# Layer norm, residual and layer-1 steps one per 128 rows, waits per bank, weight preparation spread through batch 0, new orders

## The chip, the cores and the metric

One core of one Trainium2 chip runs the kernel. The metric is the time of one execution on the device in microseconds, median of three runs. The engines are TensorE (PE; its weight loads are PEld), VectorE (DVE), ScalarE (ACT), GpSimd (POOL) and SyncE (SP), which issues the loads and stores. Each works through its own queue in order and they meet in semaphores.

## The reference, cut to what matters

Two cross-attention layers over eight batches, all in float32. x is 8 x 512 x 256, ctx 8 x 1601 x 128.

```python
# layer 0: softmax over the QUERIES (axis 1), then residual and layer norm
q = x @ Wq + bq;  k = ctx @ Wk + bk;  v = ctx @ Wv + bv
w = softmax(q @ k.T * scale, axis=1)
x = w @ v + x
x = (x - mean(x)) * rsqrt(var(x) + 1e-6) * gamma + beta
# layer 1: softmax over the KEYS (axis -1), output projection, residual
Q = x @ Wq + bq;  K = ctx @ Wk + bk;  V = ctx @ Wv + bv
out = x + (softmax(Q @ K.T * scale, axis=-1) @ V) @ Wo + bo
```

## The kernel before, in words

The projections are folded into products of weights, made once: layer 0's in `pre0`, layer 1's in `pre1`. The keys are the raw context, 13 tiles of up to 128 rows (the last has 65). Most products are made three times: an operand is split in a high half (a cast on ScalarE) and a low half (a subtraction on VectorE or GpSimd), and `split3` adds lo x hi, hi x lo and hi x hi.

Layer 0, per batch, over key tiles i = 0..12: `scores0` (TensorE), `max0` (VectorE, adds the bias and takes the row minimum of the negated scores), `exp0` (ScalarE), `recip0` (VectorE), `norm0` (ScalarE), `p0_high` (ScalarE), `p0_low` and `sum_weights` (GpSimd), `weigh0` (TensorE, accumulates in one bank). Then `weighed0`/`at0_low` split the result, `sum_rows0` gives the sum of weights per query, and for query rows: `bias_x0`, `predict`, `residual0`, `moments0`, `rsqrt_var`, `normalised`. The normalised x goes through `turn_y`, `y_turned`, `project_q1`, `q1_high`, `q1_low`.

Layer 1, per batch, over four tiles t of 128 queries: `scores1` (four chunks of 402 keys, one PSUM bank each), `rowmax1` twice, `bias1_of` (needs `bias_row1`, a product of the normalised x and a vector, one per 128 rows), `exp1` twice. When all four are done, over the 13 key tiles: `turn_p1`, `p1_turned`, `p1_low`, `weigh1`. Then `weighed1`, `project_out`, `residual1` (GpSimd) and `finish` (VectorE), and SyncE stores in two halves.

What sets the order: four lists written out by hand, one per engine. A pass of `body` runs a list with three batches in flight: c (beginning layer 0), a (layer 0 into the layer norm) and b (layer 1). `run` unrolls this over the batches, with `pre0` before the first pass and `pre1` before the second. PSUM has eight banks: `ps_l0` (four, layer 0's scores, accumulator and one for everything else) and `ps_s1` (four, layer 1). Layer 1's chunk 0 of a batch waits for the last `finish` of the batch before (line 528), and later tiles wait until the exps of the tile before have read the banks. In the last batch, tiles alternate between `ps_s1` and `ps_l0`, which layer 0 no longer needs (lines 277 and 530):

```python
return (ps_l0 if last(b) and t % 2 else ps_s1)[:].rearrange("p (k m) -> p k m", m=BANK)
before = t - 2 if last(b) else t - 1
```

The places that the change and the prediction speak of: `pre1` at lines 628 (TensorE), 810 (ScalarE), 1008 (VectorE); `scores1` 523; `bias_x0` 887; `normalised` 924; `bias_row1` 933; `finish` 971; `residual1` 1072; the loads of x and ctx 410 to 414. The helpers read in the profile as: L432, L433, L434 the three products of `split3`; L546 `turn_p1`; L872 `max0`; L736 `exp0`; L742 `norm0`; L750 `p0_high`; L1069 `p0_low`; L1062 `sum_weights`; L779 `exp1`; L951 `rowmax1`; L962 `bias1_of`; L938 `bias_row1`; L944 `q1_low`; L978 `finish`.

Of the kernel before, what the change touches and what calls it, by code (L numbers as in the profile page):

```python
# [98 lines left out]

def xattn_kernel(nc, x, ctx, wq0, bq0, wk0, bk0, wv0, bv0, gamma, beta,  # L100
# [10 lines left out]
    R0 = 4
# [1 line left out]
    SPLIT = tuple(range(MT))

    def ring0(i):

# [1016 lines left out]
```

## Time and profile before

| | us |
|---|---|
| median of 3 runs (lowest, highest) | 513.74 (513.39, 514.05) |
| the profiled execution | 513.53 |
| its span | 511.7 |
| TensorE busy | 464.3 (91%) |
| VectorE busy | 387.2 (76%) |
| ScalarE busy | 385.2 (75%) |
| GpSimd busy | 346.2 (68%) |
| mean granted clock of TensorE, share of full | 0.983 |

Busy time counts an engine's instructions; waits and the issue of transfers are not in it. The profiled execution is 1.8 us longer than its span. The eight batches overlap, so that the middle of the program repeats one pattern per batch, and only the start and the end differ from it.

### The profile page before, as it was taken

The page shows a single profiled execution, that of the slowest core. Times are in us where ns is not written, and L with a number is a line of the kernel's source. Part 1 is how long each engine was busy: PE and PEld are TensorE (multiplying, and loading weights), DVE is VectorE, ACT ScalarE, POOL GpSimd, SP SyncE. Part 2 cuts the span into 40 slices and gives each one's busy share as a digit, 9 for nine tenths or more (in the row PEclk, how much of TensorE's full clock was granted, in tenths as well). Part 3 has the DMA queues.
Part 4 walks back from the last instruction along what each step waited for, and adds up shares of the span by engine and source line. Part 5 has one row for each costly group of instructions (what it writes and reads, how often), then busy time and mean ns, then how long its engine had stood idle before and what let it go on. Part 6 is the DMA issues. An engine that isn't in the chain of part 4 may idle for free.

```text
span 511.7 us, 7981 instructions
## 1 busy us (share of the span) xinstructions
PE 464.3 (91%) x2426; PEld 381.0 (74%) x2426; DVE 387.2 (76%) x920; ACT 385.2 (75%) x798; POOL 346.2 (68%) x319
## 2 busy tenths in 40 slices
...
GB/s 241 114 0 1 1 106 0 2 2 0 7 141 2 1 1 146 3 0 1 33 115 1 1 2 147 1 0 1 66 83 0 2 3 41 0 1 10 34 0 42
DMA packets 23897, 17.31 MB, mean 34 GB/s; under 512 B 1055, under 2 KB 23854, under 8 KB 23854
## 3 DMA queue, kind: packets, MB, share of 16 engines
...
q10 hardware_dynamic: 4, 0.00, 0.0%
...
## 4 chain that ended last, share of the span: by engine, by line
PE 41%; DVE 36%; ACT 8%; issue 8%; DMA 4%; POOL 2%; SPq 0%; DVEq 0%; POOLq 0%; ACTq 0%
DVE p1T_lo L884 7%; PE ps_s L432 5%; DVE xr L938 5%; PE ps_l L432 5%; PE ps_l L433 5%; PE ps_s L434 5%; PE ps_l L434 5%; PE ps_s L433 5%; DMA x_sb<-in_x_dram 4%; DVE xr L899 4%; PE ps_s L546 4%; DVE s_sb L872 3%; DVE max L951 3%; DVE y_res L978 2%; DVE xhat L930 2%
## 5 line engine op out<-in xcount | busy, mean ns | idle before, releaser
L1069 POOL TENSOR_TENSOR p_lo<-p,p_hi 128x512 fp32r<-128x512 f32 (+1 forms) x104 | 135.2, 1307 | 83.4 <-ACT p_hi L750 83.4
L1062 POOL TENSOR_TENSOR wsum<-wsum,p 128x512 f32<-128x512 f32 (+1 forms) x88 | 115.0, 1307 | 4.6 <-ACT p L742 1.3
L736 ACT ACTIVATE p<-s_sb,min 128x512 f32<-128x512 f32 (+1 forms) x104 | 75.3, 725 | 18.8 <-DVE min L872 16.8
L884 DVE TENSOR_TENSOR p1T_lo<-ps_s,p1T_hi 128x512 fp32r<-128x512 f32 (+1 forms) x104 | 68.0, 681 | 26.7 <-ACT p1T_hi L787 26.5
L787 ACT CAST p1T_hi<-ps_s 128x512 fp32r<-128x512 f32 (+1 forms) x104 | 59.1, 585 | 30.7 <-PE ps_s L546 18.1
L872 DVE CUSTOM_DVE_ANT_0 s_sb<-ps_l,cb 128x512 f32<-128x512 f32 (+1 forms) x104 | 69.8, 683 | 12.5 <-PE ps_l L434 8.9
L742 ACT ACTIVATE p<-p,r 128x512 f32<-128x512 f32 (+1 forms) x104 | 73.1, 719 | 4.4 <-DVE r L879 3.9
L951 DVE TENSOR_REDUCE max<-ps_s 128x1 f32<-128x804 f32 x60 | 59.1, 994 | 15.7 <-PE ps_s L434 13.3
L750 ACT CAST p_hi<-p 128x512 fp32r<-128x512 f32 (+1 forms) x104 | 63.4, 618 | 1.3 <-PE ps_l L434 0.7
L546 PE MATMUL ps_s<-ident,p 128*128 128x128 f32 (+1 forms) x416 | 58.7, 279 | 5.0 <-ACT p L779 5.0
L546 PEld LDWEIGHTS ps_s<-ident,p 128*128 128x128 f32 (+1 forms) x416 | 50.4, 145 | 14.6 <-ACT p L779 7.3
L779 ACT ACTIVATE p<-ps_s,bias 128x1206 f32<-128x1206 f32 (+1 forms) x60 | 55.4, 926 | 7.5 <-DVE bias L962 7.2
L432 PE MATMUL ps_s<-ctxT_hi,qw_lo 128*128 128x402 f32 x120 | 43.7, 365 | 14.9 <-DVE qw_lo L944 10.9
L1050 POOL TENSOR_TENSOR ctx_lo<-ctx_sb,ctx_hi 128x512 fp32r<-128x512 f32 (+1 forms) x32 | 34.8, 1088 | 20.7 <-ACT ctx_hi L711 20.7
L432 PE MATMUL ps_l<-p_hi,ctx_lo 128*128 128x512 f32 (+1 forms) x104 | 46.5, 447 | 1.6 <-POOL p_lo L1069 1.3
L432 PE MATMUL ps_l<-qw_hi,ctxT_lo 128*128 128x512 f32 (+1 forms) x104 | 44.7, 430 | 2.8 <-DVE min L872 2.8
L432 PE MATMUL ps_s<-p1T_hi,ctx_lo 128*128 128x512 f32 (+1 forms) x104 | 44.0, 423 | 0.0
L434 PE MATMUL ps_l<-qw_hi,ctxT_hi 128*128 128x512 f32 (+1 forms) x104 | 41.5, 399 | 0.0
L433 PE MATMUL ps_l<-qw_lo,ctxT_hi 128*128 128x512 f32 (+1 forms) x104 | 41.4, 398 | 0.0
L434 PE MATMUL ps_s<-ctxT_hi,qw_hi 128*128 128x402 f32 x120 | 41.4, 345 | 0.0
L434 PE MATMUL ps_l<-p_hi,ctx_hi 128*128 128x512 f32 (+1 forms) x104 | 41.4, 398 | 0.0
L433 PE MATMUL ps_s<-ctxT_lo,qw_hi 128*128 128x402 f32 x120 | 41.3, 344 | 0.0
(163 smaller groups left out, 1063.8 us busy)
## 6 DMA issues: line engine op xcount, KB each, us to landing
ctx_sb<-in_ctx_dram SPq DMA_DIRECT2D x24, 256.0 KB, 4.9
...
out_dram<-y_res SPq DMA_DIRECT2D x16, 256.0 KB, 2.2
p<-in_L_xattn_Wq_dram SPq DMA_DIRECT2D x2, 256.0 KB, 3.7
...
p<-in_L_xattn_Wo_dram SPq DMA_DIRECT2D x1, 256.0 KB, 4.7
```

The lines of the kernel that those rows point to most:

```text
L432: nc.tensor.matmul(ps, w_lo, m_hi, start=start, stop=False)
L433: nc.tensor.matmul(ps, w_hi, m_lo, start=False, stop=False)
L434: return nc.tensor.matmul(ps, w_hi, m_hi, start=False, stop=stop)
L546: mm = nc.tensor.transpose(ps_turn[i % 3][0:m, t * P:(t + 1) * P], p1[:, t, i * P:i * P + m], ident[:])
L736: nc.scalar.activation(p0[0:m, ring0(i), :], s0_sb[0:m, (a.par + i) % 2, :], ACT.Exp, bias=min0[0:m, i:i + 1], scale=-1.0, accum_out=sum0[ ...
L742: nc.scalar.activation(p0[0:m, ring0(i), :], p0[0:m, ring0(i), :], ACT.Copy, scale=r0[0:m, i:i + 1]).then_inc(norm0_done, 1)
L750: nc.scalar.copy(p0_hi[0:m, split_place(i), :], p0[0:m, ring0(i), :]).then_inc(p0_hi_done, 1)
L872: nc.vector.tensor_tensor_reduce(out=s0_sb[0:m, (a.par + i) % 2, :], in0=ps_s0[0:m, (a.par + i) % 2, :], in1=cb[a.par][0:m, :], scale=-SCA ...
L884: nc.vector.tensor_tensor(p1T_lo[0:m, i % RING, :], ps_turn[i % 3][0:m, :], p1T_hi[0:m, i % RING, :].bitcast(F32), ALU.subtract).then_inc( ...
L951: nc.vector.tensor_reduce(max1[:, t, k:k + 1], s1_banks(b, t)[:, 2 * k:2 * k + 2, 0:CHUNK], AX_XY, ALU.max).then_inc(max1_done, 1)
L1062: nc.gpsimd.tensor_tensor(total, total, p0[0:m, ring0(i), :], ALU.add).then_inc(wsum_done, 1)
L1069: nc.gpsimd.tensor_tensor(p0_lo[0:m, h, :], p0[0:m, ring0(i), :], p0_hi[0:m, h, :].bitcast(F32), ALU.subtract).then_inc(p0_lo_done, 1)
```

## The change

The four lists become four tables of numbers. Every step of a batch has a place in it, the place plus 100000 times the batch number orders all steps of an engine, and the sets for the first and the last batch can add steps or move them. All four orders are new. Beside this:

- `pre1` is cut in pieces named `prepare` (4 on TensorE, 5 on ScalarE, 6 on VectorE), which have places among batch 0's steps.
- `bias_x0`, `normalised` and `bias_row1` are one step per 128 rows; `residual1` becomes `gamma_y` and `beta_y`, one each per 128 rows. Each waits for its own rows.
- In `scores1`, chunk 0 waits only for `qw1_lo`, chunks 1 and 2 each for one half of `finish`, as those are the banks that `project_out` uses. `turn_y` and ScalarE's `ctx_high` get waits of their own, which the order gave before.
- The ring of `p0` has five places in turn (before, four, and one apart for the last tile), and `exp0` waits for the low half made of the old tile and no longer for its product.
- The whole of layer 1 of the last batch has its banks in `ps_l0`, and its exps are written to the memory of x, ctx and `p0`.

```diff
80.00 3.32 PE L520 MATMUL ps_s<-xhT,a_gamma 128*128 128x512 f32 x4 tables, the one of TensorE, a line or two
-    ("weigh1", "b", 12), ("weigh0", "c", 0), ("weigh0", "c", 1), ("project_out", "b", 0), ("turn_y", "a", 0),
+TENSOR = {
+    STEADY: {
+        ("turn_x", 0): 13064, ("turn_x", 1): 19706, ("project_q0", 0): 25744, ("project_bias0", 0): 32691,
...
+    FIRST: {
+        ("prepare", 0): 31059, ("prepare", 1): 37222, ("prepare", 2): 46948, ("prepare", 3): 60771,
+    },
+    LAST: {},
80.00 3.32 PE L520 MATMUL ps_s<-xhT,a_gamma 128*128 128x512 f32 x4 how the order is made
+def program(places, batches):
+    steps = []
+    for n in range(batches):
+        own = {**places[STEADY], **(places[FIRST] if n == 0 else places[LAST] if n == batches - 1 else {})}
+        steps += [(SLOT * n + at, n, name, i) for (name, i), at in own.items() if at is not None]
+    return [(n, name, i) for _, n, name, i in sorted(steps)]
80.00 3.32 PE L520 MATMUL ps_s<-xhT,a_gamma 128*128 128x512 f32 x4 rings and banks
-    R0 = 4
+    R0 = 5
...
+    def ring0(a, i):
+        return (MT * a.n + i) % R0
...
-        def s1_banks(b, t):
-            return (ps_l0 if last(b) and t % 2 else ps_s1)[:].rearrange("p (k m) -> p k m", m=BANK)
+        def s1_banks(b):
+            return (ps_l0 if last(b) else ps_s1)[:].rearrange("p (k m) -> p k m", m=BANK)
...
+        def p1_rows(b, t):
+            if last(b):
+                return (x_flat, ctx_flat[1], p0_flat, ctx_flat[0])[t][:, 0:M]
+            return p1[:, t, :]
80.00 3.32 PE L520 MATMUL ps_s<-xhT,a_gamma 128*128 128x512 f32 x4 scores1 (TensorE)
                 if i == 0:
-                    if not first(b):
-                        pe.wait_ge(o_done, 2 * b.n)
                     pe.wait_ge(qw1_lo_done, b.n + 1)
-                before = t - 2 if last(b) else t - 1
-                if before >= 0 and k in (0, len(chunks) - 1):
-                    pe.wait_ge(exp1_done, 2 * (TB * b.n + before) + (1 if k == 0 else 2))
+                if t == 0 and k in (1, 2) and not first(b) and not last(b):
+                    pe.wait_ge(o_done, 2 * (b.n - 1) + k)
+                if t and k in (0, len(chunks) - 1):
+                    pe.wait_ge(exp1_done, 2 * (TB * b.n + t - 1) + (1 if k == 0 else 2))
80.00 3.32 PE L520 MATMUL ps_s<-xhT,a_gamma 128*128 128x512 f32 x4 ctx_high and exp0 (ScalarE)
                 act.wait_ge(ctxT_ps, GROUPS * a.n + g + 1)
+                if a.n >= 2:
+                    act.wait_ge(s1_ps, KC * TB * (a.n - 1))
...
-                if (held := before0(a, i)) is not None:
-                    back, last = held
-                    act.wait_ge(pv0_ps, MT * (a.n - back) + last + 1)
-                    act.wait_ge(wsum_done, summed(a.n - back, last))
+                k = MT * a.n + i - R0
+                if k >= 0:
+                    act.wait_ge(wsum_done, k + 1)
+                if k >= 0 and k // MT in split:
+                    act.wait_ge(p0_lo_done, halves(batch(k // MT), k % MT) + 1)
80.00 3.32 PE L520 MATMUL ps_s<-xhT,a_gamma 128*128 128x512 f32 x4 the weights of layer 1 (ScalarE; TensorE's and VectorE's pieces are cut likewise)
-            def pre1():
-                act.wait_ge(wv_loaded, 16 * 3)
-                nc.scalar.copy(wv0_hi[:], wv0_sb).then_inc(wv0_hi_done, 1)
...
+            def prepare(_, i):
+                if i == 0:
+                    act.wait_ge(wv_loaded, 16 * 3)
+                    nc.scalar.copy(wv0_hi[:], wv0_sb).then_inc(wv0_hi_done, 1)
+                elif i == 1:
+                    act.wait_ge(wT_turned, 3)
+                    nc.scalar.copy(wqT[1].rearrange("p h e -> p (h e)"), s1_bank(0)).then_inc(wT_copied, 1)
...
80.00 3.32 PE L520 MATMUL ps_s<-xhT,a_gamma 128*128 128x512 f32 x4 per 128 rows (VectorE)
-            def bias_row1(b, _):
-
+            def bias_row1(b, t):
                 dve.wait_ge(row1_made, MADE)
-                dve.wait_ge(xhat_done, TB * (b.n + 1))
-                for t in range(TB):
-                    nc.vector.tensor_tensor_reduce(out=xr[:, t, :], in0=xhat[:, t, :], in1=u1_gamma[:], scale=1.0,
...
+                dve.wait_ge(xhat_done, TB * b.n + t + 1)
+                nc.vector.tensor_tensor_reduce(out=xr[:, t, :], in0=xhat[:, t, :], in1=u1_gamma[:], scale=1.0,
...
80.00 3.32 PE L520 MATMUL ps_s<-xhT,a_gamma 128*128 128x512 f32 x4 per 128 rows (GpSimd)
+            def gamma_y(b, t):
+                pool.wait_ge(row1_made, MADE)
+                pool.wait_ge(xhat_done, TB * b.n + t + 1)
+                pool.wait_ge(out_free[t // 2], 16 * (b.n + 1))
+                nc.gpsimd.tensor_tensor(y_res[:, t, :], xhat[:, t, :], gamma_row[:], ALU.mult).then_inc(y_part_done, 1)
+            def beta_y(b, t):
+                pool.wait_ge(y_part_done, TB * b.n + t + 1)
+                nc.gpsimd.tensor_tensor(y_res[:, t, :], y_res[:, t, :], betaob_row[:], ALU.add).then_inc(y_res_done, 1)
```

How the instructions stand now at four places.

TensorE at the start, before: the block of `pre1` behind batch 0's third context transpose (L570, L574, L632 turn weights; L580 vectors; L588, L639, L643 make products).

```order
L440 MATMUL ps_l<-ident,ctx_sb 128x128 [waits ctx_loaded0_2,ctxT_lo_done]
L440 MATMUL ps_l<-ident,ctx_sb 128x128 x3
L570 MATMUL ps_s<-ident,p 128x128 [waits w_loaded1]
L570 MATMUL ps_s<-ident,p 128x128 x3
L574 MATMUL ps_s<-ident,p 128x128 x2
L632 MATMUL ps_s<-ident,p 128x128 [waits wv_loaded]
L632 MATMUL ps_s<-ident,p 128x128
L580 MATMUL ps_s<-ident,vec_rows 128x5 [waits cols_loaded1]
L580 MATMUL ps_s<-ident,vec_rows 128x5
L588 MATMUL ps_s<-p 128x128 [waits wT_copied]
L588 MATMUL ps_s<-p 128x128 x3
L639 MATMUL ps_s<-p 128x256 [waits reps_done]
```

And now: the same transposes between `project_q0` and `project_bias0` (L480, waiting for `qw0_lo_done`) of batch 0.

```order
L628 MATMUL ps_s<-ident,p 128x128 [waits w_loaded1]
L628 MATMUL ps_s<-ident,p 128x128 x3
L632 MATMUL ps_s<-ident,p 128x128 x2
L692 MATMUL ps_s<-ident,p 128x128 [waits wv_loaded]
L692 MATMUL ps_s<-ident,p 128x128
L638 MATMUL ps_s<-ident,vec_rows 128x5 [waits cols_loaded1]
L638 MATMUL ps_s<-ident,vec_rows 128x5
L480 MATMUL ps_l<-xT_hi,u_lo 128x512 [waits qw0_lo_done]
L481 MATMUL ps_l<-xT_lo,u_hi 128x512
L482 MATMUL ps_l<-xT_hi,u_hi 128x512
```

The turning of the weights moved ahead of all scores of batch 0.

ScalarE at the start, before: behind `pre0`'s copies comes `q0_high` (L721), the bias, the context's high half, the first exp.

```order
L806 COPY small<-ps_l 128x2 [waits small_ps]
L703 CAST ctxT_hi<-ps_l 128x512 [waits ctxT_ps]
L721 ACTIVATE qw_hi<-ps_l,small 128x512 [waits qw0_ps,small_sb]
L726 ACTIVATE cb<-ps_l,small 128x512 [waits cb_ps]
L703 CAST ctxT_hi<-ps_l 128x512 [waits ctxT_ps]
L736 ACTIVATE p,sum<-s_sb,min 128x512 [waits s0_read]
```

And now: `prepare` 0 (L873) ahead of `q0_high` (L779), `prepare` 1 and 2 behind it.

```order
L866 COPY small<-ps_l 128x2 [waits small_ps]
L761 CAST ctxT_hi<-ps_l 128x512 [waits ctxT_ps]
L873 CAST wv_hi<-p 128x256 [waits wv_loaded,small_sb]
L779 ACTIVATE qw_hi<-ps_l,small 128x512 [waits qw0_ps]
L876 COPY p<-ps_s 128x512 [waits wT_turned]
L878 COPY p<-ps_s 128x256 [waits wT_turned]
L879 COPY p<-ps_s 128x256
L784 ACTIVATE cb<-ps_l,small 128x512 [waits cb_ps]
L882 COPY a_sb<-ps_s 128x256 [waits made_ps]
L883 COPY p<-ps_s 128x256
L797 ACTIVATE p,sum<-s_sb,min 128x512 [waits s0_read]
```

The first exp now has six more copies ahead of it.

VectorE at a handover, before: the last two of four `bias_row1` (L938), `finish` (L978) of the batch before, `q1_low` (L944).

```order
L938 ISA c 128x1
L938 ISA xr,c<-xhat,u_gamma,c_const 128x256
L938 ISA c 128x1
L978 SCALAR_TENSOR_TENSOR y_res<-ps_s,r,y_res 128x256 [waits out_ps,y_res_done,r1_done]
L978 SCALAR_TENSOR_TENSOR y_res<-ps_s,r,y_res 128x256
L872 ISA s_sb,min<-ps_l,cb 128x512 [waits s0_ps,ident_done,exp0_done]
L872 ISA min 128x1
L978 SCALAR_TENSOR_TENSOR y_res<-ps_s,r,y_res 128x256 [waits out_ps]
L978 SCALAR_TENSOR_TENSOR y_res<-ps_s,r,y_res 128x256
L843 TENSOR_TENSOR ctxT_lo<-ps_l,ctxT_hi 128x512 [waits ctxT_hi_done]
L879 RECIPROCAL r<-sum 128x1 [waits exp0_done] x2
L944 SCALAR_TENSOR_TENSOR qw_lo<-ps_s,scaled,qw_hi 128x512 [waits qw1_hi_done]
```

And now: two `bias_row1` (L992) between the normalisation (L986) and `finish` (L1031).

```order
L986 TENSOR_SCALAR xhat<-xr,mv,rstd 128x256 [waits y_part_done,xhT_ps,rstd_done] x4
L992 ISA xr,c<-xhat,u_gamma,c_const 128x256 [waits xhat_done,row1_made]
L992 ISA c 128x1
L992 ISA xr,c<-xhat,u_gamma,c_const 128x256 [waits xhat_done,row1_made]
L992 ISA c 128x1
L1031 SCALAR_TENSOR_TENSOR y_res<-ps_s,r,y_res 128x256 [waits out_ps,y_res_done,r1_done]
L1031 SCALAR_TENSOR_TENSOR y_res<-ps_s,r,y_res 128x256
L933 ISA s_sb,min<-ps_l,cb 128x512 [waits s0_ps,ident_done,exp0_done]
L933 ISA min 128x1
L940 RECIPROCAL r<-sum 128x1 [waits exp0_done] x2
L1031 SCALAR_TENSOR_TENSOR y_res<-ps_s,r,y_res 128x256 [waits out_ps,y_res_done]
L1031 SCALAR_TENSOR_TENSOR y_res<-ps_s,r,y_res 128x256
```

The other two stand behind the second query tile's bias, after `q1_low`; a `max0` has come in front of `q1_low`.

TensorE at the end, before: scores of the last batch, from tile 0's last product on; the buffer names have their numbers.

```order
L434 MATMUL ps_s1<-ctxT_hi1,qw1_hi 128x402
L432 MATMUL ps_l0<-ctxT_hi1,qw1_lo 128x402
L433 MATMUL ps_l0<-ctxT_lo1,qw1_hi 128x402
L434 MATMUL ps_l0<-ctxT_hi1,qw1_hi 128x402
L432 MATMUL ps_l0<-ctxT_hi1,qw1_lo 128x402
```

And now, from the same product on.

```order
L482 MATMUL ps_l0<-ctxT_hi1,qw1_hi 128x402
L480 MATMUL ps_l0<-ctxT_hi1,qw1_lo 128x402 [waits exp1_done]
L481 MATMUL ps_l0<-ctxT_lo1,qw1_hi 128x402
L482 MATMUL ps_l0<-ctxT_hi1,qw1_hi 128x402
L480 MATMUL ps_l0<-ctxT_hi1,qw1_lo 128x402
```

Tile 1 had other banks and no wait; it has the same banks now and waits for tile 0's exp.

## Rows read from the trace of the kernel before

**Rows 1.** Busy time per stretch: stretch, its length, then each engine, clock, DMA.

```profile
30.00:60.00 30.00, 22.87 (x105) 17.90 (x106) 16.25 (x42) 21.21 (x48) 23.46 (x20) 0.94 0.00 1
...
120.00:420.00 300.00, 288.40 (x1547) 239.90 (x1547) 253.50 (x601) 248.00 (x515) 225.50 (x204) 1.00 0.11 32
...
475.00:489.00 14.00, 9.52 (x49) 8.70 (x50) 9.30 (x16) 7.71 (x16) 5.62 (x8) 1.00 0.01 2
```

**Rows 2.** Start: the last of three weight loads, then starts of instructions (start, length).

```profile
p<-in_L_xattn_Wo_dram SPq DMA_DIRECT2D x1, 256.0 KB, 4.7
...
11.97 0.43 SPq L401 DMA_DIRECT2D p<-in_L_xattn_Wo_dram  x1
...
15.64 0.69 ACT L721 ACTIVATE qw_hi<-ps_l,small 128x512 fp32r<-128x512 f32 x1 [2.69 <-PE ps_l L434]
...
35.22 2.07 PE L588 MATMUL ps_s<-p 128*128 128x128 f32 x8 [5.25 <-ACT p L817]
...
38.58 1.03 PE L643 MATMUL ps_s<-p 128*128 128x256 f32 x4
```

**Rows 3.** GpSimd and ScalarE in batch 0, by time; ScalarE's tile from 22.79 to 24.62.

```profile
22.25 1.28 POOL L1050 TENSOR_TENSOR ctx_lo<-ctx_sb,ctx_hi 128x512 fp32r<-128x512 f32 x1 [20.75 <-ACT ctx_hi L711]
...
24.80 2.57 POOL L1069 TENSOR_TENSOR p_lo<-p,p_hi 128x512 fp32r<-128x512 f32 x2 [1.26 <-ACT p_hi L750]
...
27.31 1.30 POOL L1059 TENSOR_TENSOR wsum<-p 128x512 f32<-128x512 f32 x1
...
22.79 0.71 ACT L742 ACTIVATE p<-p,r 128x512 f32<-128x512 f32 x1
...
24.62 0.72 ACT L742 ACTIVATE p<-p,r 128x512 f32<-128x512 f32 x1
```

**Rows 4.** From the row sums to the first layer-1 scores, by time.

```profile
64.81 1.07 PE L496 MATMUL ps_l<-ones,wsum 128*128 128x1 f32 x8 [0.32 <-POOL wsum L1062]
...
75.79 2.33 DVE L930 TENSOR_SCALAR xhat<-xr,mv,rstd 128x256 f32<-128x256 f32 x4
...
80.00 3.32 PE L520 MATMUL ps_s<-xhT,a_gamma 128*128 128x512 f32 x4
...
83.70 0.68 DVE L872 CUSTOM_DVE_ANT_0 s_sb<-ps_l,cb 128x512 f32<-128x512 f32 x1
...
86.65 0.45 PE L432 MATMUL ps_s<-ctxT_hi,qw_lo 128*128 128x402 f32 x1 [1.25 <-DVE qw_lo L944]
```

**Rows 5.** Who waited for whom, TensorE, 120 to 420 us: total, times, longest.

```profile
PE ps_s L432 <- DVE qw_lo L944: 6.7, 5, 1.3
...
PE ps_l L448 <- DMA x_sb<-in_x_dram: 3.4, 5, 0.9
```

**Rows 6.** Line L938 (min/median/max ns), then a handover: `finish` and the transpose of x.

```profile
L938 DVE CUSTOM_DVE_ANT_0 xr<-xhat,u_gamma,c_const x32: 480/1480/1507, 78.3 to 470.8; 128x256 f32<-128x256 f32 x32
...
253.53 0.86 DVE L978 SCALAR_TENSOR_TENSOR y_res<-ps_s,r,y_res 128x256 f32<-128x256 f32 x2
...
259.27 0.63 PE L448 MATMUL ps_l<-ident,x_sb 128*128 128x128 f32 x4 [0.88 <-DMA x_sb<-in_x_dram]
```

**Rows 7.** The end, by time: scores, bias, exp, next scores in the same banks.

```profile
475.07 0.42 PE L432 MATMUL ps_s<-ctxT_hi,qw_lo 128*128 128x402 f32 x1 [1.66 <-DVE qw_lo L944]
...
479.15 1.27 ACT L779 ACTIVATE p<-ps_s,bias 128x1206 f32<-128x1206 f32 x1 [5.01 <-DVE bias L962]
...
480.56 0.45 PE L432 MATMUL ps_s<-ctxT_hi,qw_lo 128*128 128x402 f32 x1 [0.86 <-ACT p L779]
...
488.87 1.54 PE L546 MATMUL ps_s<-ident,p 128*128 128x128 f32 x6 [3.55 <-ACT p L779]
```

**Rows 8.** Stretches as in rows 1; the number behind GpSimd's is the granted clock.

```profile
62.00:66.00 4.00, 2.80 (x15) 1.81 (x13) 1.64 (x7) 4.00 (x10) 4.00 (x5) 0.96 0.00 0
...
66.00:70.00 4.00, 3.43 (x8) 2.38 (x9) 3.80 (x10) 2.43 (x7) 2.25 (x2) 0.50 0.04 10
...
489.00:492.00 3.00, 3.00 (x15) 2.90 (x16) 1.21 (x2) 1.45 (x3) 0.00 (x0) 0.50 0.00 0
```

More of the change, by code:

```diff
@@ L110, in xattn_kernel, with halves, half0, half_before @@
     RING = 4
[L111 removed]
+    R0 = 5
     RH = 3
[L113 to L143 removed]
+    def ring0(a, i):
+        return (MT * a.n + i) % R0
+    split = [n for n in range(B) if n not in IN_FLOAT]
+    def halves(a, i):
+        return MT * split.index(a.n) + i
+    def half0(a, i):
+        return halves(a, i) % RH
+    def half_before(a, i):
+        k = halves(a, i) - RH
+        return 0 if k < 0 else MT * split[k // MT] + k % MT + 1
     assert L == P and T == BANK and EC == 2 and TB == 4 and B % 2 == 0
@@ L162, in last @@
     def last(bt):
[L163 removed]
+        return bt.n == B - 1
     with ExitStack() as stack:
@@ L421, in body @@
                                  ).then_inc(out_free[h], 16)
-            run(body, (pre0, pre1), sp)
+            pre0()
+            for n in range(B):
+                if n + 2 < B:
+                    sp.wait_ge(xbias_done, TB * (n + 1))
+                    load_x(batch(n + 2))
+                    for g in range(GROUPS):
+                        load_ctx(batch(n + 2), g, after=True)
+                store(batch(n))
             for h in range(2):
@@ L684, in _ @@
             steps = {f.__name__: f for f in (
-                turn_x, project_q0, project_bias0, turn_ctx, scores0, weigh0, sum_rows0, predict, turn_y, project_q1, scores1, turn_p1, weigh1, project_out)}
-            def body(a, b, c, done=()):
-                for step, (name, who, i) in enumerate(TENSOR_ORDER):
-                    bt = {"a": a, "b": b, "c": c}[who]
-                    if bt and (name, i) not in done:
-                        if name in MISC:
-                            misc_read(step, a, b, c, done)
-                        steps[name](bt, i)
-            run(body, (pre0, pre1), pe)
+                turn_x, project_q0, project_bias0, turn_ctx, scores0, weigh0, sum_rows0, predict, turn_y, project_q1, scores1,
+                turn_p1, weigh1, project_out, prepare)}
+            pre0()
+            held = None
+            for n, name, i in after_start(TENSOR):
+                if name in MISC:
+                    if held:
+                        misc_read(*held)
+                    held = name, batch(n), i
+                steps[name](batch(n), i)
         @blk.scalar
@@ L838, in _ @@
+            steps = {f.__name__: f for f in (
+                x_turned, q0_high, bias0, ctx_high, ctx_split, exp0, norm0, p0_high, weighed0, y_turned, q1_high, exp1,
+                p1_turned, weighed1, prepare)}
+            pre0()
+            for n, name, i in after_start(SCALAR):
+                steps[name](batch(n), i)
         @blk.vector
```

487 lines of the change are left out of this document (244 added, 243 removed), and 107 rows, old and new, of tables (GPSIMD, GPSIMD_ORDER, SCALAR, SCALAR_ORDER).

## The prediction

> **What bounds the kernel now.** I read the stretches first, then who waits for whom in the steady part, then the order of time at the start, at one handover and at the end. The stretches [rows 1] are to show where TensorE is not working: in the 300 us from 120 to 420 it is busy for 288.4, and its mean granted clock is full. So the middle is TensorE's, and only 11.6 us of it can go. The rest of its idle time lies at the ends: it is busy for 22.87 of the 30 us from 30 on, and for 9.52 of the 14 from 475 on. The change keeps the arithmetic, so it can only move idle time and half-clock time. I sum it in four places.
>
> **The start, up to the first layer-1 scores (86.65 us).** Before, all of layer 1's weight work stands in a block (`pre1`) behind batch 0's sixth scores. TensorE stops in it for 5.25 us, because ScalarE's copies are behind its softmax queue, and goes on at 35.22 [rows 2]. Now `prepare` stands earlier, in four pieces.
> It costs at first. ScalarE's first step is now the copy of Wv, which waits for `wv_loaded`, all three loads. The last of them is issued at 11.97 and takes 4.7 us: 16.7. Behind it stands `q0_high`, which ran at 15.64 [rows 2]; with the copy of 0.4 it now starts at 17.1, so 1.5 later. TensorE then does `prepare` 1 (8 products of 128 columns and 4 of 256; `pre1` took 3.36 for them, mostly at half clock, from 35.22 to 38.58 [rows 2], and I take 1.9) ahead of the first scores, which start 3.3 later than before. ScalarE's first context split now follows two exps and one normalisation, so GpSimd starts at 26.9 instead of 22.25 [rows 3].
> From there GpSimd sets the pace of batch 0. It has 13 low halves, 12 sums and 4 splits; two take 2.51 from start to start [rows 3], so 28 x 1.255 + 0.45 for the short split = 35.6. Before, from 22.25 to the row sums' start at 64.81 [rows 4] it is 42.5 for the same work but the last low half: about 8 us of it was waiting for ScalarE in the block and after it. In the new order ScalarE is always ahead of GpSimd by my walk (a normalisation, an exp and a high half take 1.83, from 22.79 to 24.62, against GpSimd's 2.51 for a tile [rows 3]), and the fifth place of `p0` lets an exp start when the low half is made and not when the product is. With 0.3 of waits the last sum ends at 26.9 + 35.6 + 0.3 = 62.8, and the last low half 2.6 before that, so the product that closes batch 0's attention is done by 61 and `at0_low` is out of the way. From the row sums on, four bias rows of 0.6, residual, a `max0` of 0.7, moments, residual, moments, `max0` bring the normalisation to 71.9, 9.1 after the last sum (75.79 before [rows 4]; residual and moments of a half take about 2 together). Behind it VectorE had four `bias_row1` of 1.4 start to start before it came to `max0` at 83.7 [rows 4]; now two stand there and two are behind the second bias. That is 2.8 less and one `max0` of 0.7 more: VectorE is free for `q1_low` at 79.1. TensorE's product for q1 took 3.32 at half clock [rows 4]; with that again it ends at 80.5, at full clock at 78.6. ScalarE 0.6, VectorE 0.75: the first scores start between 80 and 82, I take 81.0, 5.6 sooner than 86.65 [rows 4]. One more layer-0 score of 0.7 stands ahead of them and is done with. Sum: **-6.3** (bounds -9 and 0).
>
> **The handovers (batches 1 to 6).** In the steady part TensorE waits at two steps [rows 5]: for `qw1_lo` 6.7 us in 5 times, and for x 3.4 in 5. Both come from VectorE's queue after the normalisation: four `bias_row1`, whose median is 1.48 where the shortest is 0.48 [rows 6], then finish, max, finish, the context's low half, `q1_low`. Now it is two `bias_row1`, finish, max, finish, max, low half. From the end of weigh1's last product I count on TensorE 8.4 us of work to the first scores in both orders, and 10.2 from start to start before, against 9.25 now (VectorE: 4.7 to the end of the second bias row, 0.8, 0.7, 0.2, 0.8, 0.7, 0.6, 0.75). That is -0.95. The wait per bank takes nothing further off: scores must wait for `qw1_lo`, which VectorE makes behind finish in both orders. The x load stands on SyncE behind the store of the batch before, which waits for finish; finish ended at 254.4 and TensorE got x at 259.27 [rows 6]. Finish is 1.45 sooner, the scores 0.95, so the wait of 0.88 shrinks by 0.45. Against it: ScalarE's `ctx_high` now waits until the scores of two batches back are all out. It stands ahead of them by 2.2 us of TensorE, and behind it on ScalarE are the last context split, an exp of layer 0 and the exps of the fourth query tile, for which turn_p1 waits. The tile's maximum takes 1.45 after the scores anyway, so most of it is hidden; I charge 0.3. That is 0.95 + 0.45 - 0.3 = 1.1 at five of them, and at the sixth, which has no x to wait for and hides half of the charge, 0.8. Sum: -5.5 - 0.8 = **-6.3** (bounds -11, which is all the idle time of rows 1's middle, and +6, a further microsecond at each).
> Split steps (bias rows, normalisations, gamma and beta rows) are as many instructions as before; GpSimd's are now spread and may wait up to a microsecond for the store, and GpSimd is busy for 225.5 of the middle's 300 [rows 1]: nothing.
>
> **Batch 6's scores, with only batch 7 to fill in (420 to 475).** Fillers of 2.8, 2.2 and 2.1 us stand in the three gaps instead of 2.8, 2.1 and 1.5: **-0.5** (bounds -1 and 0).
>
> **The end.** Before, batch 7's four query tiles alternate between two sets of four banks: `before = t - 2`. Now the whole layer has `ps_l0` alone, and tile t waits for the exps of tile t - 1. What that cycle takes can be read from the same trace, since tiles 0 and 2 share a set: scores start at 475.07, the first exp runs from 479.15, and tile 2 starts at 480.56 [rows 7]. One round is 5.49 us. Four tiles: 3 x 5.49 + 6.03 (scores to the end of both exps) = 22.5, where 488.87 - 475.07 = 13.8 [rows 7]. Nothing else is left to fill the gaps: TensorE's steps ahead are in the same order as before, turn_y still follows project_out. That is **+8.7**, and no other edit touches it.
> In such a round TensorE works 2.5 us of 5.5. The granted clock fell to 0.50 in 66 to 70 after 62 to 66, where TensorE was busy 2.80 of 4, eight of its products only one column wide; and to 0.50 behind 488.87 [rows 8], after an idle time of 3.55 [rows 7]. Twelve products at 0.183 start to start then take 1.85 us longer. I take two of the four rounds at half clock: **+3.7** (bounds 0 and 7.4).
> The Trainium skill (TensorE: Matmul & The Clock Gate, section on HAM oscillation) warns of loops whose every round waits and so starts cold, and ties this to idle gaps longer than these. By it the gaps here, 3.0 us, would leave the clock at its upper level.
>
> **Sum.** The profiled execution took 513.53 us for a span of 511.7. 513.53 - 6.3 - 6.3 - 0.5 + 8.7 + 3.7 = 512.8. The median of the runs is 513.74, so 0.2 must be allowed between the two. A measurement of this kernel can tell about 0.2% (1.0 us) from no change.
>
> **Rivals.**
> 1. The clock holds at the end. For it: TensorE idles 0.86 us ahead of 480.56 [rows 7] and the clock of that stretch stays at 1.00 [rows 1]; against it, the row of 66 to 70. 512.8 - 3.7 = 509.1.
> 2. The handover waits go nearly altogether and the clock is as in my sum: the new order leaves 0.2 instead of 1.1 at each. For it: TensorE has enough work there, 8.4 us; against it, VectorE's chain of 9.25 is longer. 512.8 - 5.4 = 507.4.
> 3. All four last rounds run at 1.2 GHz. 512.8 + 3.7 = 516.5: slower. It decides at the first round: once tile 1's twelve products take 4 us instead of 2.2, tiles 2 and 3 do.
> 4. ScalarE's new wait in `ctx_high` holds its queue, the exps of the fourth tile and with them turn_p1 come late in each of six batches. It takes the whole gain there and 1 us more: 512.8 + 6.3 + 1.2 = 520.3. It decides if the wait is over 1.4 us.
> 5. The start gains nothing, because GpSimd's start, 4.6 us later, goes through: the waits of 8 us that I let vanish come back, from the loads or from ScalarE. 519.1.
>
> **Chances.** My sum 0.36 (own range 508.5 to 517), rival 1 0.20, rival 2 0.12, rival 3 0.13, rival 4 0.09, rival 5 0.10. The bound for faster is 512.5, for slower 514.6. My sum's 0.36 splits 0.13, 0.11, 0.12. Faster: 0.13 + 0.20 + 0.12 = 0.45; slower: 0.12 + 0.13 + 0.09 + 0.10 = 0.44, of which I give 0.02 to no change, since rivals 3 and 5 can meet the gains of rival 2: 0.42; same: 0.13. The range from 504.5 to 519.5 takes in rivals 1 to 3, 5 and most of what the bounds add.
>
> **What would show it.** In the new profile the first layer-1 scores start near 81 us and GpSimd's first split near 27. TensorE's wait for `qw_lo` is under 1 us at a handover, and TensorE is busy for 293 or more of the 300 us of the middle. The last batch's scores and exps take 22 us or more, in four rounds with 3 us of idle time in each, and the clock shows 0.50 in part of them. The forecast is wrong if the middle gained nothing, if the last rounds overlap something, or if the start's first scores come after 85.

## The result: 6.0% slower, 546.58 us

| | before | after |
|---|---|---|
| median (lowest, highest) | 513.89 us (513.39 to 517.71, 4 runs) | 546.58 us (545.95 to 549.48, 4 runs) |
| ratio to before, 95% interval | | 1.060 (1.055 to 1.065) |
| span of the profiled run | 511.7 | 543.9 |
| TensorE busy, mean granted clock | 464.3, 0.983 | 474.6, 0.959 |

The forecast was 512.8 with a range to 519.5. The start of the first layer-1 scores of each batch (the product of `ctxT_hi` with `qw_lo`) cuts both spans at the same places, so that the difference can be laid out and summed:

| stretch | before | after | difference | forecast |
|---|---|---|---|---|
| start to the first layer-1 scores | 86.65 | 87.64 | +1.0 | -6.3 |
| six batches from there | 339.5 (56.6 each) | 358.8 (59.8 each) | +19.3 | -6.3 |
| batch 6's to batch 7's scores | 49.0 | 48.1 | -0.8 | -0.5 |
| batch 7's scores to the end | 36.6 | 49.3 | +12.7 | +12.4 |

Of the -6.3 in the first row, 0.7 is a layer-0 score that was to be done sooner; it lies behind this cut, and the scores themselves were forecast at 81.0. The end came as forecast. The first two rows did not, and all of the 32.9 us between the forecast (-0.7) and the result (+32.2) lie there.

The stretches of the kernel after, in the columns of [rows 1]:

```profile
30.00:60.00 30.00, 22.50 (x91) 15.46 (x90) 13.91 (x35) 23.52 (x50) 27.38 (x23) 0.94 0.00 1
60.00:90.00 30.00, 21.66 (x89) 15.78 (x88) 25.69 (x55) 18.38 (x38) 20.78 (x19) 0.77 0.16 46
120.00:420.00 300.00, 277.86 (x1458) 229.46 (x1457) 248.44 (x564) 236.42 (x493) 220.57 (x195) 0.99 0.11 32
```

TensorE's idle time in the middle grew from 11.6 to 22.1 us, some 2 us a batch of the 3.2 by which a batch grew. Who it waited for there, the answer to [rows 5]:

```profile
PE ps_s L572 <- DVE xhat L986: 11.1, 5, 3.1
PE ps_s L604 <- DVE p1T_lo L945: 8.8, 5, 1.8
PE ps_l L480 <- DVE ctxT_lo L904: 1.2, 2, 0.6
PE ps_s L480 <- DVE qw_lo L998: 0.6, 2, 0.3
```

The two waits that the change was forecast to shorten are gone: `qw1_lo` from 6.7 to 0.6, x from 3.4 to none. Two that did not exist have come, both for VectorE: `turn_y` for the normalisation (L986), and `turn_p1` for a low half of the attention (L945). What VectorE did shows in the shortest, median and longest time of one instruction in ns. After:

```profile
L986 DVE TENSOR_SCALAR xhat<-xr,mv,rstd x32: 405/1352/1381, 76.3 to 488.6; 128x256 f32<-128x256 f32 x32
L958 DVE SCALAR_TENSOR_TENSOR xr<-bv_row,rowsum,x_sb x32: 471/954/3709, 66.4 to 479.7; 128x256 f32<-128x256 f32 x32
L992 DVE CUSTOM_DVE_ANT_0 xr<-xhat,u_gamma,c_const x32: 474/481/1495, 80.4 to 505.7; 128x256 f32<-128x256 f32 x32
```

And before (`normalised` and `bias_x0`; `bias_row1` is in [rows 6]):

```profile
L930 DVE TENSOR_SCALAR xhat<-xr,mv,rstd x32: 403/410/1361, 75.8 to 469.0; 128x256 f32<-128x256 f32 x32
L899 DVE SCALAR_TENSOR_TENSOR xr<-bv_row,rowsum,x_sb x32: 471/474/1489, 66.2 to 459.5; 128x256 f32<-128x256 f32 x32
```

The slow form has moved to the front. Before, three of four `bias_row1` took 1.48 us (shortest 0.48) and the normalisation 0.41. Now the normalisation takes 1.35; of the four `bias_row1` the two right behind it still take 1.49 and 1.48 at most handovers, and the two that come later 0.48. From the first normalisation to the end of the second bias row it is 7.0 to 7.1 us in each of the first seven batches, and was 3.4 before at the handovers. The instructions are the same, on the same shapes. GpSimd beside them says why. GpSimd at a handover of after:

```profile
250.84 0.71 POOL L1144 TENSOR_TENSOR rstd<-var_eps,neg_half 128x2 f32<-128x2 f32 x1 [1.35 <-DVE var_eps L979]
254.37 0.69 POOL L1144 TENSOR_TENSOR rstd<-var_eps,neg_half 128x2 f32<-128x2 f32 x1 [2.83 <-DVE var_eps L979]
255.03 3.85 POOL L1128 TENSOR_TENSOR p_lo<-p,p_hi 128x512 fp32r<-128x512 f32 x3
258.83 1.31 POOL L1121 TENSOR_TENSOR wsum<-wsum,p 128x512 f32<-128x512 f32 x1
260.11 1.32 POOL L1107 TENSOR_TENSOR ctx_lo<-ctx_sb,ctx_hi 128x512 fp32r<-128x512 f32 x1
```

VectorE and TensorE in the same microseconds:

```profile
255.11 5.18 DVE L986 TENSOR_SCALAR xhat<-xr,mv,rstd 128x256 f32<-128x256 f32 x4
260.21 1.49 DVE L992 CUSTOM_DVE_ANT_0 xr<-xhat,u_gamma,c_const 128x256 f32<-128x256 f32 x1
...
260.35 1.09 PE L572 MATMUL ps_s<-ident,xhat 128*128 128x128 f32 x8 [3.14 <-DVE xhat L986]
```

Four normalisations take 5.18 us, one GpSimd instruction each (3.85 for three, 1.31 for the fourth). This handover is the longest. GpSimd began first here, 255.03 against 255.11; at the other five from batch 1 on VectorE did, the first normalisation took 0.41 and the four 4.25 or 4.26. The same place in the kernel before:

```profile
245.95 1.38 DVE L930 TENSOR_SCALAR xhat<-xr,mv,rstd 128x256 f32<-128x256 f32 x4
...
247.74 2.77 POOL L1069 TENSOR_TENSOR p_lo<-p,p_hi 128x512 fp32r<-128x512 f32 x2 [1.62 <-ACT p_hi L750]
```

GpSimd stood idle, as its next low half waited for ScalarE, and the four took 1.38. When it began, the turn was `bias_row1`'s to be slow. The new GpSimd order has three low halves ready there.

The other wait, `turn_p1`'s, begins at `bias_x0`, again with GpSimd beside it:

```profile
242.74 3.68 DVE L958 SCALAR_TENSOR_TENSOR xr<-bv_row,rowsum,x_sb 128x256 f32<-128x256 f32 x4 [0.23 <-DVE rowsum L951]
...
242.87 0.95 POOL L1139 TENSOR_TENSOR y_res<-y_res,betaob_row 128x256 f32<-128x256 f32 x1
243.79 0.91 POOL L1135 TENSOR_TENSOR y_res<-xhat,gamma_row 128x256 f32<-128x256 f32 x1
244.66 1.48 POOL L1118 TENSOR_TENSOR wsum<-p 128x512 f32<-128x512 f32 x1
```

One by one the four take 0.49, 0.96, 0.96 and 1.51 us: from the second on, each is as long as the GpSimd instruction beside it. Before, the four took 2.67 there. The low half for which TensorE waits stands behind them on VectorE.

The waits are not all of it. TensorE's granted clock fell to 1.2 GHz at three of the six handovers (at 200.5, 320.0 and 439.5 us), and before at none:

```profile
199.43 1.09 PE L572 MATMUL ps_s<-ident,xhat 128*128 128x128 f32 x8 [1.99 <-DVE xhat L986]
200.36 1.73 PE L620 MATMUL ps_s<-w_sb,at 128*128 128x256 f32 x4
```

The same four products of L620 take 1.03 us at 261.28, where the clock stayed at 2.4 GHz.

The start shows the collision twice, in the answers to [rows 3] and [rows 4]:

```profile
26.16 1.28 POOL L1107 TENSOR_TENSOR ctx_lo<-ctx_sb,ctx_hi 128x512 fp32r<-128x512 f32 x1 [24.65 <-ACT ctx_hi L769]
...
66.42 4.90 DVE L958 SCALAR_TENSOR_TENSOR xr<-bv_row,rowsum,x_sb 128x256 f32<-128x256 f32 x4
...
76.29 4.23 DVE L986 TENSOR_SCALAR xhat<-xr,mv,rstd 128x256 f32<-128x256 f32 x4
```

They took 2.38 (`bias_x0`, the four from 66.22) and 2.33 before. Of the 4.90, the first `bias_x0` alone has 3.71, while GpSimd ran three instructions in a row (66.11 to 69.84); so it can be more than one.

### The profile page after: what moved, and what is told of

Same layout as the page of the kernel before. It is cut to its first block, busy times and chain, and to the rows that moved or that the text cites. A ratio compares the mean times of both kernels' runs of the same rounds, so it can differ in the third digit from the quotient of the medians.

```text
span 543.9 us, 8058 instructions
## 1 busy us (share of the span) xinstructions
PE 474.6 (87%) x2426; PEld 387.9 (71%) x2426; DVE 401.8 (74%) x920; ACT 384.6 (71%) x798; POOL 351.7 (65%) x319
## 4 chain that ended last, share of the span: by engine, by line
PE 63%; DVE 17%; issue 6%; ACT 6%; POOL 3%; SPq 2%; DMA 2%; DVEq 0%; ACTq 0%; POOLq 0%
PE ps_l L480 10%; PE ps_l L482 9%; PE ps_l L481 9%; PE ps_s L480 7%; PE ps_s L482 6%; PE ps_s L481 6%; PE ps_s L604 5%; DVE xr L958 4%; PE ps_s L620 2%; DVE xhat L986 2%; DVE p1T_lo L945 2%; DVE s_sb L933 2%; PE ps_s L580 2%; DVE max L1005 1%; ACT p L797 1%
## 5 line engine op out<-in xcount | busy, mean ns | idle before, releaser
L1005 DVE TENSOR_REDUCE max<-ps_s 128x1 f32<-128x804 f32 x56 | 55.7, 995 | 26.0 <-PE ps_s L482 22.5
L945 DVE TENSOR_TENSOR p1T_lo<-ps_s,p1T_hi 128x512 fp32r<-128x512 f32 (+1 forms) x91 | 60.3, 682 | 17.8 <-ACT p1T_hi L847 17.8
L847 ACT CAST p1T_hi<-ps_s 128x512 fp32r<-128x512 f32 (+1 forms) x91 | 52.1, 585 | 29.5 <-PE ps_s L482 14.9
L604 PE MATMUL ps_s<-ident,p 128*128 128x128 f32 (+1 forms) x364 | 51.5, 274 | 12.4 <-DVE p1T_lo L945 11.1
L1107 POOL TENSOR_TENSOR ctx_lo<-ctx_sb,ctx_hi 128x512 fp32r<-128x512 f32 (+1 forms) x32 | 35.7, 1114 | 37.2 <-ACT ctx_hi L769 37.2
L604 PEld LDWEIGHTS ps_s<-ident,p 128*128 128x128 f32 (+1 forms) x364 | 43.1, 142 | 20.9 <-DVE p1T_lo L945 12.8
L839 ACT ACTIVATE p<-ps_s,bias 128x1206 f32<-128x1206 f32 (+1 forms) x56 | 52.1, 933 | 5.2 <-DVE bias L1015 4.9
L480 PE MATMUL ps_l<-qw_hi,ctxT_lo 128*128 128x512 f32 (+1 forms) x104 | 48.3, 465 | 2.4 <-DVE ctxT_lo L904 1.9
L480 PE MATMUL ps_l<-p_hi,ctx_lo 128*128 128x512 f32 (+1 forms) x104 | 46.9, 451 | 1.7 <-POOL p_lo L1128 1.7
L480 PE MATMUL ps_s<-ctxT_hi,qw_lo 128*128 128x402 f32 x112 | 40.6, 362 | 2.6 <-ACT p L839 1.9
L482 PE MATMUL ps_l<-qw_hi,ctxT_hi 128*128 128x512 f32 (+1 forms) x104 | 42.7, 410 | 0.0
L1135 POOL TENSOR_TENSOR y_res<-xhat,gamma_row 128x256 f32<-128x256 f32 x32 | 24.9, 778 | 25.5 <-DMA out_dram<-y_res 25.5
L482 PE MATMUL ps_l<-p_hi,ctx_hi 128*128 128x512 f32 (+1 forms) x104 | 41.3, 397 | 0.0
L481 PE MATMUL ps_l<-p_lo,ctx_hi 128*128 128x512 f32 (+1 forms) x104 | 41.1, 395 | 0.0
L480 PE MATMUL ps_s<-p1T_hi,ctx_lo 128*128 128x512 f32 (+1 forms) x91 | 38.8, 427 | 0.0
```

The costliest lines, as they stand in the source:

```text
L480: nc.tensor.matmul(ps, w_lo, m_hi, start=start, stop=False)
L481: nc.tensor.matmul(ps, w_hi, m_lo, start=False, stop=False)
L482: return nc.tensor.matmul(ps, w_hi, m_hi, start=False, stop=stop)
L604: mm = nc.tensor.transpose(ps_turn(b, i)[0:m, t * P:(t + 1) * P], p1_rows(b, t)[:, i * P:i * P + m], ident[:])
L945: nc.vector.tensor_tensor(p1T_lo[0:m, i % RING, :], ps_turn(b, i)[0:m, :], p1T_hi[0:m, i % RING, :].bitcast(F32), ALU.subtract).then_inc(p ...
L1005: nc.vector.tensor_reduce(max1[:, t, k:k + 1], s1_banks(b)[:, 2 * k:2 * k + 2, 0:CHUNK], AX_XY, ALU.max).then_inc(max1_done, 1)
```

## The experiments

Theory A: VectorE's `normalised`, `bias_x0` and `bias_row1` cannot run beside an instruction of GpSimd, and the new orders put GpSimd's ready work beside those for which TensorE waits. Theory B: TensorE's own new order has too little ahead of `turn_y`. Theory C came later: the new orders have a value of their own, once the collisions are out of the way. Ratios are to the kernel before on the same chip, where its median was 517.6 to 517.8; the traces of before and after are from a chip where before took 513.9, so that stretches of a run can be half a microsecond a batch longer than those of before and after for that alone.

### A pause of GpSimd over the normalisations

```diff
             def rsqrt_var(a, h): ...
+            def hold_norm(a, _):          # a step behind rsqrt_var 1
+                pool.wait_ge(xhat_done, TB * (a.n + 1))
```

> Theory A: GpSimd's instructions and VectorE's that read two tensors of the on-chip memory (or one, in the fast form of the normalisation) take turns, and the new GpSimd order has three low halves ready just when the four normalisations run. The kernel of after with one wait more: GpSimd stands still behind its second power of the variance until the four normalisations are made. By A the normalisation falls from a median of 1.35 us to 0.41, TensorE's wait at turn_y for it from 11.1 us in 5 times to under 2, and the time falls by some 2.8 us a batch in six handovers and 1.9 at the start: 528 us (522 to 534). Theory B: it is TensorE's own order, which has too little ahead of turn_y; VectorE is late because of what it does before. Then the pause only costs GpSimd 2 us a batch: 546 to 550.

521.98 us, 1.008 (1.005 to 1.011): 5.2% of before less than after. The normalisation:

```profile
L986 DVE TENSOR_SCALAR xhat<-xr,mv,rstd x32: 405/409/413, 76.5 to 463.5; 128x256 f32<-128x256 f32 x32
```

The wait of `turn_y` is gone, and a single kind is left in the middle:

```profile
PE ps_s L604 <- DVE p1T_lo L945: 10.6, 6, 1.8
```

A wait added to GpSimd took the span from 543.9 to 520.7. Theory B is out: TensorE's order was not touched. The gain is more than the 18 us expected; a batch fell from 59.8 to 56.0, and the first layer-1 scores from 87.64 to 85.15. Beside the wait, the falls of the clock in the middle are gone (mean granted clock 1.00 from 120 to 420), which the expectation had not counted. The end took 51.3 us where it took 49.3: its last rounds ran at 1.2 GHz for longer.

### A second pause, over `bias_x0`

```diff
+            def hold_bias(a, _):          # behind the next batch's first ctx_low
+                pool.wait_ge(xbias_done, TB * (a.n + 1))
```

> As the kernel with the pause behind the power, and a second pause: GpSimd waits for the four bias rows of bias_x0 too. By theory A those fall from 3.68 us for four to about 1.9 in the middle and from 4.90 to 2.4 at the start, and with them the wait of turn_p1 for p1_low (8.8 us in 5 times) to under 3: another 8 to 12 us less than with one pause, 518 us (513 to 526), and the first layer-1 scores at 83 us or earlier where they stand at 87.64. By theory B nothing, or 2 to 10 us more than with one pause, as GpSimd loses another 2 us a batch.

508.71 us, 0.982 (0.978 to 0.985): faster than before by a little under 2%, and below the 513 to 526 expected. First layer-1 scores at 82.46, a batch 54.2, and in the middle TensorE is busy for 298.66 of 300:

```profile
120.00:420.00 300.00, 298.66 (x1588) 249.53 (x1587) 245.62 (x630) 256.75 (x540) 242.01 (x218) 1.00 0.12 34
```

Four `bias_x0` take 1.67 us where they took 3.68, so that the low halves of the attention queued behind them on VectorE come in time, and the wait of `turn_p1` goes. GpSimd's wait for the store ahead of `gamma_y`, 17.4 us in 5 times in after and new with the change, has gone as well without having been touched.

### The second pause alone

The step `hold_bias` as above, and no `hold_norm`.

> The kernel of after with the pause for bias_x0 alone. If the two pauses act on places of their own, it gives what it gave on top of the other: 13 us less than after, 1.034 of before (1.028 to 1.042). The wait of turn_p1 for p1_low goes, that of turn_y for the normalisation stays at 2 to 3 us a batch. If the late normalisation swallows it, under 5 us: above 1.050.

536.06 us, 1.035 (1.029 to 1.042). The waits that are left in the middle:

```profile
PE ps_s L572 <- DVE xhat L986: 12.5, 5, 3.5
PE ps_l L480 <- DVE ctxT_lo L904: 1.2, 2, 0.6
PE ps_s L480 <- DVE qw_lo L998: 0.6, 2, 0.3
```

Each pause takes away its own wait. 1.060 less 0.025 for this one and 0.052 for the other is 0.983, and both gave 0.982.

### The collision planted in the kernel before

```diff
                 nc.gpsimd.tensor_tensor(rstd[:, two, :], ..., ALU.pow).then_inc(rstd_done, 1)
+                if h == 1:
+                    for k in range(3):    # 128 x 512, nothing uses the sum
+                        nc.gpsimd.tensor_tensor(spare_out[:], <ident, four times>, <ident, four times>, ALU.add)
```

> The kernel before, with three additions more on GpSimd per batch (128 x 512, about 1.26 us each, of values that nothing uses) behind the second power of the variance, where it was idle for 1.62 us. By theory A they slow VectorE's four normalisations from 1.38 us to 3.5 to 5, TensorE gets turn_y and qw1_lo 2 to 3 us later in each batch, and the time rises by 12 to 20 us: 526 to 534. By theory B GpSimd has room (it waits for 65 us for ScalarE between 120 and 420 us), so 514 to 516.

542.69 us, 1.048 (1.042 to 1.053), more than the 526 to 534 expected, and close to after. VectorE, GpSimd and TensorE at a handover:

```profile
256.30 3.69 DVE L932 TENSOR_SCALAR xhat<-xr,mv,rstd 128x256 f32<-128x256 f32 x4
...
256.43 3.40 POOL L1096 TENSOR_TENSOR spare_out<-ident 128x512 f32<-128x512 f32 x3
...
260.04 1.09 PE L516 MATMUL ps_s<-ident,xhat 128*128 128x128 f32 x8 [1.52 <-DVE xhat L932]
```

The normalisations went from 1.38 to 3.69 us with nothing changed but GpSimd's idle time. A batch takes 60.5 us, 3.9 more than before. TensorE waits for the normalisation (7.6 us in 5 times between 120 and 420) and, further on, for a layer-0 maximum that stands behind it on VectorE (7.8 in 5), and its mean granted clock there is 0.97 where it was 1.00. The wait for `qw1_lo` is 6.7 as before, and that for x has shrunk to 1.9.

### Three memsets instead

```diff
-                        nc.gpsimd.tensor_tensor(spare_out[:], ...)
+                        nc.gpsimd.memset(spare_out[:], 0.0)
```

> The kernel before with three GpSimd memsets (128 x 512, written and never read) in the place of the three additions of the busy variant. If what collides is the reading of the on-chip memory, the memsets leave VectorE's normalisations at 0.41 us and the time rises by what GpSimd itself loses, under 4 us: 0.998 to 1.008. If an instruction of GpSimd holds the shared way whatever it does, the normalisations rise to the memsets' length as they did to the additions' (3.69 us for four) and the time with them, as far as the memsets are as long: 1.02 to 1.05.

538.15 us, 1.038 (1.030 to 1.045).

VectorE and GpSimd at a handover:

```profile
257.87 3.29 DVE L932 TENSOR_SCALAR xhat<-xr,mv,rstd 128x256 f32<-128x256 f32 x4
...
257.98 1.76 POOL L1096 MEMSET spare_out<- 128x512 f32 x3
```

So GpSimd need not read to hold up the normalisation: 1.76 us of memsets and one low half (which started at 259.71) made 1.38 into 3.29. The Trainium skill (SBUF — State Buffer, section Who interferes with whom) says the same of `tensor_scalar`: in its form with two ports it takes a pair of ports that GpSimd shares, whoever comes first holds it for a whole instruction and the other waits. The normalisation is a `tensor_scalar`; that it runs in this form no trace shows, but its times agree, one GpSimd instruction's length per normalisation, and the first of four is spared where VectorE began first. The first three of the four take 0.79, 0.69 and 0.69 us beside memsets of some 0.55, and the fourth, beside the low half, 1.35. Of VectorE instructions with two inputs there, such as `bias_x0` and `bias_row1`, the page says that they collide only with GpSimd instructions that read; these kernels show them colliding with additions and subtractions (0.48 against 1.48 us), and no run shows what a memset does to them.

### The end, with two sets of banks again

```diff
-            return (ps_l0 if last(b) else ps_s1)[:]...
+            return (ps_l0 if last(b) and t % 2 == 0 else ps_s1)[:]...
-                if t and k in (0, len(chunks) - 1):
-                    pe.wait_ge(exp1_done, 2 * (TB * b.n + t - 1) + (1 if k == 0 else 2))
+                back = 2 if last(b) else 1
+                if last(b) and t == 1 and k == 0:
+                    pe.wait_ge(o_done, 2 * b.n)
+                if t >= back and k in (0, len(chunks) - 1):
+                    pe.wait_ge(exp1_done, 2 * (TB * b.n + t - back) + (1 if k == 0 else 2))
```

> The kernel of after, but the last batch's query tiles alternate between the two sets of four banks and wait for the exps of two tiles back, as before. The prediction's term for it: 8.7 for the rounds and 3.7 for the clock, so 534.2 us (531 to 538), with turn_p1 about 14 us behind the first scores. If the single set is not what makes the end 12.7 us longer (the exps, or VectorE's maxima, set the round), it gains under 4: 543 or more.

534.6 us, 1.032 (1.029 to 1.035), near the 534.2 expected, with `turn_p1` 14.0 us behind the first scores. By the ratios that is 14.6 us less than after, by the two profiles 10.8. From the last batch's scores to the end it takes 37.2 us, and 36.6 before. In after the rounds are seen at the first score of each tile, the answer to [rows 7]:

```profile
494.55 0.45 PE L480 MATMUL ps_l<-ctxT_hi,qw_lo 128*128 128x402 f32 x1 [1.56 <-DVE qw_lo L998]
...
500.05 0.45 PE L480 MATMUL ps_l<-ctxT_hi,qw_lo 128*128 128x402 f32 x1 [3.05 <-ACT x_sb L839]
...
506.79 0.45 PE L480 MATMUL ps_l<-ctxT_hi,qw_lo 128*128 128x402 f32 x1 [3.05 <-ACT ctx_sb L839]
...
513.47 0.45 PE L480 MATMUL ps_l<-ctxT_hi,qw_lo 128*128 128x402 f32 x1 [3.05 <-ACT p L839]
```

The first round takes 5.50 us (forecast 5.49), the next two 6.74 and 6.68. The stretches, whose last but two column is the granted clock, show what the rest is:

```profile
494.50:500.00 5.50, 2.46 (x12) 2.12 (x12) 2.42 (x4) 1.36 (x3) 4.13 (x6) 1.00 0.00 0
500.00:506.00 6.00, 3.69 (x12) 3.14 (x12) 3.07 (x7) 1.18 (x3) 0.00 (x0) 0.72 0.01 3
506.00:512.00 6.00, 3.63 (x12) 3.06 (x12) 2.55 (x6) 1.31 (x4) 0.00 (x0) 0.72 0.00 0
512.00:518.00 6.00, 3.50 (x12) 2.95 (x12) 2.01 (x3) 1.93 (x4) 0.00 (x0) 0.71 0.00 0
518.00:523.00 5.00, 2.41 (x12) 2.42 (x12) 1.07 (x3) 2.92 (x6) 0.00 (x0) 0.50 0.00 0
```

The clock falls from 2.4 to 1.2 GHz part way through each of the last three rounds, behind 3.05 us without work in each.

### Both pauses and both sets

The steps `hold_norm` and `hold_bias`, and the banks as in the last experiment.

> The kernel of after with both pauses of GpSimd and the last batch's scores in two sets of banks. The two do not touch the same place: 0.9819 of before with the pauses, less 0.0283 that the two sets gave (1.0602 to 1.0319), is 0.954 (0.950 to 0.962), about 490 us where before takes 513.9. If the single set gave something back that only the pauses show (the last batch's layer 1 starting earlier), it stays above 0.970.

495.26 us, 0.956 (0.951 to 0.961): 13.4 us less than with one set, close to the 2.8% (14.6 us) that the two sets gave without the pauses: the two do not touch each other.

### The kernel before, with a pause

```diff
                 nc.gpsimd.tensor_tensor(rstd[:, two, :], ..., ALU.pow).then_inc(rstd_done, 1)
+                if h == 1:
+                    pool.wait_ge(c1_done, TB * (a.n + 1))
```

> The kernel before, with one pause: GpSimd stands still behind the second power until the four normalisations and the four bias_row1 are made. Its normalisations are fast already (0.41 us), its bias rows are not (median 1.48, shortest 0.48). By theory A they fall to 0.48, VectorE reaches q1_low 3 us sooner, the wait for qw1_lo (1.34 a batch) goes and part of the wait for x: 0.975 to 0.988 of before. Theory C, that the gain over before lies in the new order and the pauses only undo the new order's harm: before gains nothing by it, 0.995 to 1.01, as GpSimd loses 2 us a batch.

495.27 us, 0.956 (0.951 to 0.961), a larger gain than expected, from one line. In the middle TensorE's idle time went from 11.6 to 1.6 us, so the wait for x went whole and not in part. Its `bias_row1`, to be read against [rows 6], and its stretch in the middle, against [rows 1]:

```profile
L938 DVE CUSTOM_DVE_ANT_0 xr<-xhat,u_gamma,c_const x32: 479/481/486, 77.3 to 450.4; 128x256 f32<-128x256 f32 x32
```

```profile
120.00:420.00 300.00, 298.37 (x1602) 251.71 (x1601) 248.03 (x628) 259.97 (x543) 237.61 (x216) 1.00 0.12 34
```

Who GpSimd waited for from 120 to 420 us: it stands idle for the pause (second row) and loses nothing, because it then waits less for ScalarE (first row; 65.5 us in 39 times in before):

```profile
POOL p_lo L1069 <- ACT p_hi L750: 35.4, 27, 2.9
POOL p_lo L1069 <- DVE c L938: 18.8, 6, 3.1
```

Theory C falls too. The old orders with one pause are as fast as the new ones with two pauses and the old banks: first scores at 82.90 and 82.53, a batch 53.8 and 54.2, the end 36.7 and 36.8 us. The spreading of the weight work, the steps per 128 rows and the waits per bank, taken together, bring nothing that can be measured beside this; no run took them one by one.

### A longer pause

On top of both pauses and both sets:

```diff
-("rsqrt_var", 1): 170853 ... ("p0_low", 1): 76247      (in a batch's frame, 176247 of the batch ahead)
+("rsqrt_var", 1): 170853 ... ("p0_low", 1): 70840
             def hold_norm(a, _):
-                pool.wait_ge(xhat_done, TB * (a.n + 1))
+                pool.wait_ge(c1_done, TB * a.n + 2)
```

> The kernel of after with both pauses and two sets of banks, changed in two places: the pause behind the second power lasts until the first two bias_row1 are made too, and GpSimd makes the second low half of the next batch before that power, where it waits 1.72 us. TensorE is busy for 298.6 of the 300 us from 120 to 420 already, so the middle can give 1 us; at the start (two bias rows of 1.5 that fall to 0.48, ahead of q1_low) 1 to 2, and at the last batch 1 at most. 0.956 less 0.004 to 0.007: 0.949 to 0.952 of before. If GpSimd has become the one that is waited for, it is 0.956 or more.

494.29 us, 0.956 (0.950 to 0.962): no difference to be told, where 0.949 to 0.952 was expected. The profile shows 1.4 us gained at the start (first scores at 81.14), 0.8 in the six batches, and 1.2 lost at the end (38.0 us from the last scores). What cost the end that is open.

## Why the prediction was wrong

- **The end, +8.7 and +3.7.** Right in mechanism and size: 26.0 us from the first scores to `turn_p1` (494.55 to 520.59), where 22.5 + 3.7 was forecast. The clock fell in part of three rounds, not in the whole of two, and that both come to nearly the same is luck: the twelve products took 3.5 to 3.7 us in three rounds instead of 2.46, where two rounds were priced at 1.85 more. The forecast of a fall leaned on the row of 66 to 70 and on the fall behind 3.55 us in before; by the rule of the Trainium skill (TensorE: Matmul & The Clock Gate, section on HAM oscillation) the 3.05 us gaps here would have left it at its upper level, and they did not; nor did waits of 1.99 us at three handovers. Here the measurement decides.
- **Batch 6, -0.5.** -0.8.
- **The start, -6.3.** GpSimd did begin at 26.16 (26.9 forecast) and did set the pace, though its last sum ended 2.1 us later than 62.8, as it waited 2.2 us for ScalarE where 0.3 was forecast. What failed is the walk of VectorE behind it: "four bias rows of 0.6" took 4.90 together, and the normalisations 4.23 instead of the 2.33 of the trace before. That is 4.4 us, and with the 2.1 it makes 6.5 of the 6.6 between 81.0 and 87.64. With the collisions out of the way the first scores start at 81.14, the 81.0 of the forecast.
- **The handovers, -6.3.** The failed step is "VectorE: 4.7 to the end of the second bias row". From the first normalisation to there it took 7.0 us (255.11 to 262.1), 5.18 of it the normalisations. Beside two bias rows of 1.48, the 4.7 has room for little more than their 1.38 of the trace before, as if that belonged to the instruction; it belonged to GpSimd's 1.62 us of idle time beside it. A second failure has no term in the sum at all: `bias_x0`, whose collisions make TensorE wait 1.8 us a batch at `turn_p1`; the pause over it alone gave 2.5% of before. The third part of the miss is the clock at three handovers, of which the sum for the handovers had nothing. The figures stood in [rows 6]: the same instruction at 480 and at 1480 ns. That row asked what runs beside it, and the prediction took it for the order of things.
- **"GpSimd's ... nothing."** This sentence let the change go by. GpSimd's low share of busy time was taken as room. Its steps were moved to where VectorE's critical ones are, and there each VectorE instruction that meets it lasts about as long as GpSimd's own (1.35 beside 1.28 us), and once 3.71.
- **The rivals.** None named VectorE slowed by GpSimd. Rival 4 (ScalarE's new wait) and rival 5 (the start gains nothing) had the right sign. Rival 4's wait is in the profile, but small, and no exp keeps TensorE waiting in the middle: `ACT ctxT_hi L761 <- PE ps_s L482: 1.7, 5, 0.4`, where it was to decide from 1.4 us on. Of the 8 us of waits in rival 5, 2.2 came back.
